# Decoder layer on one core: the last two steps of the feed-forward network interleaved by token tile, with the last layer norm and the store done tile by tile

## What is computed

```python
x = _layernorm(x + attention(x, Wq, bq, Wk, bk, Wv, bv, Wo, bo))      # 16 heads, rope, causal
x = _layernorm(x + cross(x, ctx, Wq, bq, Wk, bk))                     # softmax(q k^T) over the context, applied to x
gate = einsum('bsd,hd->bsh', x, w_gate)                               # d = 512, h = 2048
up = einsum('bsd,hd->bsh', x, w_up)
gated = silu(gate) * up
x = _layernorm(x + einsum('bsh,dh->bsd', gated, w_down))
```

## Time and profile before

| What | Value |
|---|---|
| Median of 3 runs | 1050.85 us (1048.11, 1050.85, 1050.95) |
| The profiled execution's own time | 1048.29 us |
| Its span | 1046.5 us |
| TensorE busy in the span | 94% |
| Mean granted TensorE clock | 0.978 of full speed |
| VectorE, ScalarE, GpSimd busy | 60%, 47%, 34% |

### The profile page before, as it was taken

How to read it: one execution, slowest core, us unless ns; L and a number is a source line. 1 busy time by engine, 2 the same in 40 slices (tenths; PEclk the granted TensorE clock), 3 DMA queues, 4 the chain that set the end, 5 groups by cost and what they waited for, 6 DMA issues and landing times.

```text
span 1046.5 us, 15709 instructions
## 1 busy us (share of the span) xinstructions
PE 981.5 (94%) x5416; PEld 794.5 (76%) x5416; DVE 630.3 (60%) x1344; ACT 493.5 (47%) x1075; POOL 352.3 (34%) x353
## 2 busy tenths in 40 slices
PE   7688999999999868899999999999999999999995
PEld 5556777777777656688888788888788888788884
DVE  5577788878778766545544475544565444653343
ACT  5476767777767654344432334432334432333330
POOL 2566646655756521213111132012132112131112
PEclk9899999999999979899999999999999999999998
DMA  6966676855868730262222143222252221242301
GB/s 219 255 152 168 171 183 158 229 142 145 242 158 191 186 120 1 91 230 91 73 79 91 61 175 148 91 73 80 78 207 98 91 91 61 91 171 92 111 9 41
DMA packets 44862, 134.53 MB, mean 129 GB/s; under 512 B 5232, under 2 KB 5360, under 8 KB 41968
## 3 DMA queue, kind: packets, MB, share of 16 engines
q1 hardware_dynamic: 44784, 133.52, 42.1%
HBM read 104.14 MB, written 25.17 MB: 124 GB/s over the span
## 4 chain that ended last, share of the span: by engine, by line
PE 79%; ACT 6%; DVE 5%; issue 5%; POOL 2%; DMA 2%; SPq 1%; POOLq 0%; DVEq 0%; ACTq 0%
PE pu L523 17%; PE pg L523 17%; PE pd L523 16%; PE pj L478 11%; PE pj L523 5%; PE pv L514 4%; PE ps L489 3%; PE pa L502 2%; ACT prob L678 2%; PE pb L502 2%; DVE prob L874 2%; PE pj L529 1%; ACT pT L685 1%; PE pj L476 1%; DMA ks<-qk_scratch 1%
## 5 line engine op out<-in xcount | busy, mean ns | idle before, releaser
L1191 POOL TENSOR_TENSOR g_lo<-gated,g_hi 128x512 fp32r<-128x512 f32 x64 | 82.5, 1289 | 439.8 <-ACT g_hi L769 439.8
L678 ACT ACTIVATE prob<-prob,nmax 128x512 f32<-128x512 f32 (+3 forms) x256 | 143.7, 562 | 114.4 <-DVE nmax L874 114.2
L874 DVE CUSTOM_DVE_ANT_0 prob<-ps,mask 128x512 f32<-128x512 f32 (+3 forms) x256 | 122.8, 484 | 79.8 <-PE ps L489 76.0
L980 DVE TENSOR_TENSOR dn_lo<-f_raw,dn_hi 128x512 fp32r<-128x512 f32 x64 | 51.2, 801 | 121.2 <-ACT dn_hi L753 121.2
L489 PE MATMUL ps<-ks,qs 128*128 128x256 f32 (+2 forms) x256 | 107.0, 420 | 13.5 <-DMA ks<-qk_scratch 8.0
L1001 DVE SCALAR_TENSOR_TENSOR half<-th,pg 128x512 f32<-128x512 f32 x64 | 43.9, 687 | 104.4 <-ACT th L760 104.4
L523 PE MATMUL pd<-dn_hi,g_hi 128*128 128x512 f32 x256 | 101.2, 395 | 0.2 <-POOL g_lo L1191 0.2
L760 ACT ACTIVATE th<-pg 128x512 f32<-128x512 f32 x64 | 38.3, 598 | 131.6 <-PE pg L523 131.6
L523 PE MATMUL pd<-dn_lo,g_hi 128*128 128x512 f32 x256 | 99.8, 390 | 0.0
L523 PE MATMUL pd<-dn_hi,g_lo 128*128 128x512 f32 x256 | 99.6, 389 | 0.0
L769 ACT CAST g_hi<-gated 128x512 fp32r<-128x512 f32 x64 | 39.7, 620 | 120.4 <-DVE gated L1008 120.4
(11 more groups left out here) (162 smaller groups left out, 2226.4 us busy)
## 6 DMA issues: line engine op xcount, KB each, us to landing
f_raw<-in_w_ffn SPq DMA_DIRECT2D x64, 768.0 KB, 4.3
qs<-qk_scratch SPq DMA_DIRECT2D x64, 256.0 KB, 4.8
ks<-qk_scratch SPq DMA_DIRECT2D x64, 256.0 KB, 7.8
qk_scratch<-qk_hi SPq DMA_DIRECT2D x32, 256.0 KB, 2.0
qk_scratch<-raw SPq DMA_DIRECT2D x32, 256.0 KB, 2.1
res<-in_x SPq DMA_DIRECT2D x4, 1024.0 KB, 4.9
x_scratch<-res SPq DMA_DIRECT2D x4, 1024.0 KB, 5.8
x<-x_scratch SPq DMA_DIRECT2D x4, 1024.0 KB, 4.8
```

The costliest lines, as they stand in the source:

```text
L678: act.activation(prob[:, t % PROBS, 0:w], prob[:, t % PROBS, 0:w], ACT.Exp, bias=nmax[:, n % 2, i:i + 1], scale=-1.0, accum_out=rsum[:, n ...
L874: dve.tensor_tensor_reduce(prob[:, t % PROBS, 0:w], ps[:, t % 2, 0:w], mask[:, S - w:S], -D ** -0.5, 3e38, ALU.add, ALU.min, accum_out=nma ...
L980: dve.tensor_tensor(dn_lo[:, i % 2, :], f_raw[i % NR][:, 2 * KT * P:], dn_hi[:, i % 2, :].bitcast(F32), ALU.subtract).then_inc(dnlo_done, 1)
L1191: pool.tensor_tensor(g_lo[:, i % 2, :], gated[:], g_hi[:, i % 2, :].bitcast(F32), ALU.subtract).then_inc(glo_done, 1)
```

## The change

Four edits, all at the end of the fourth sequence.

1. PE's order. The loop of steps ends at i = 61. Then `hidden` of steps 62 and 63 run one behind the other, then `down(61)`, and then the down products of steps 62 and 63 in turn, token tile by token tile: 3 matmuls of step 62 and 3 of step 63 finish a tile and raise `tile_full`.
2. Banks and buffers. The gate and up products of step 63 go to the two banks of `pj`, which nothing uses any more at that time, and not to `pg` and `pu`. The halves of the gated activation and of the down weights of step 63 have buffers of their own, `last_hi` and `last_lo`. `gu_half(63)` moves from the midst of step 62 to the end of step 61, on ACT and DVE.
3. Layer norm. The sum and the moments of a tile wait for that tile's `tile_full` and not for the whole `d_full`. POOL makes -mean*rstd (`nmr2`) for tiles 0 to 2 by one more instruction each, and ACT normalizes these three tiles; DVE normalizes only tile 3.
4. Store. SP issues one store of 256 KB for each tile in place of one of 1 MB.

```diff
+    last_hi, last_lo, nmr2 = sb("last_hi", [P, 2, S], F32R), sb("last_lo", [P, 2, S], F32R), sb("nmr2", [P, ST])
...
+    def gate_bank(i):
+        return pj[:, 0, :] if i == STEPS - 1 else pg[:]
+    def up_bank(i):
+        return pj[:, 1, :] if i == STEPS - 1 else pu[:]
+    def gated_halves(i):
+        return (last_hi[:, 0, :], last_lo[:, 0, :]) if i == STEPS - 1 else (g_hi[:, i % 2, :], g_lo[:, i % 2, :])
+    def down_halves(i):
+        return (last_hi[:, 1, :], last_lo[:, 1, :]) if i == STEPS - 1 else (dn_hi[:, i % 2, :], dn_lo[:, i % 2, :])
...
@@ SP @@
-            sp.wait_ge(ln_done[1], ST * (b + 1))
-            sp.dma_start(out[b * P:(b + 1) * P, :], fin[:]).then_inc(out_done, 16)
-        sp.wait_ge(out_done, 16 * B)
+            if not last:
+                sp.wait_ge(ln_done[1], ST * (b + 1))
+                sp.dma_start(out[b * P:(b + 1) * P, :], fin[:]).then_inc(out_done, 16)
+        for s in range(ST):
+            if s < ST - 1:
+                sp.wait_ge(tile_done, s + 1)
+            else:
+                sp.wait_ge(ln_done[1], ST * (B - 1) + 1)
+            sp.dma_start(out[(B - 1) * P:B * P, s * E:(s + 1) * E], fin[:, s, :]).then_inc(out_done, 16)
+        sp.wait_ge(out_done, 16 * (B - 1 + ST))
...
@@ PE @@
+        def last_down(i, s):
+            if s == 0:
+                pe.wait_ge(dnlo_done, i + 1)
+                pe.wait_ge(glo_done, i + 1)
+            cols = slice(s * P, (s + 1) * P)
+            return three(pd[:, s, :], 1, lambda k: [g[:, cols] for g in gated_halves(i)],
+                         lambda k: down_halves(i), False, i == STEPS - 1)
-        for i in range(1, STEPS):
+        for i in range(1, STEPS - 2):
             hidden(i, 0)
             hidden(i, 1)
...
             down(i - 1)
-        down(STEPS - 1)
+        for i in (STEPS - 2, STEPS - 1):
+            hidden(i, 0)
+            hidden(i, 1)
+        down(STEPS - 3)
+        for s in range(ST):
+            last_down(STEPS - 2, s)
+            last_down(STEPS - 1, s).then_inc(tile_full, 1)
...
@@ ACT, step (DVE's the same) @@
-            if i < STEPS - 1:
+            if i < STEPS - 2:
                 gu_half(i + 1)
...
             if i < STEPS - 1:
                 dn_half(i + 1)
+            if i == STEPS - 3:
+                gu_half(i + 2)
...
@@ ACT, behind the last step @@
+        for s in range(ST - 1):
+            act.wait_ge(nmr2_done, s + 1)
+            act.activation(fin[:, s, :], fin[:, s, :], ACT.Identity, bias=nmr2[:, s:s + 1],
+                           scale=rstd2[1][:, s, :]).then_inc(tile_done, 1)
...
@@ DVE @@
         def finished(b, s):
             if s == 0:
                 dve.wait_ge(fin_in, 16 * (b + 1))
+            if b == B - 1:
+                dve.wait_ge(tile_full, s + 1)
+            elif s == 0:
                 dve.wait_ge(d_full, HT * (b + 1))
...
-        for s in range(ST):
-            normalized(B - 1, 1, fin, s)
+        normalized(B - 1, 1, fin, ST - 1)
...
@@ POOL @@
             root(B - 1, 1, s)
+            if s < ST - 1:
+                pool.wait_ge(rstd2_done[1], ST * (B - 1) + s + 1)
+                pool.tensor_scalar(nmr2[:, s:s + 1], mv2[1][:, s, 0:1], rstd2[1][:, s, :], -1.0, ALU.mult, ALU.mult).then_inc(nmr2_done, 1)
```

More of the change, by code:

```diff
@@ L588, in hidden @@
                     pe.wait_ge(max_done, SCORES)
-                else:
+                elif i < STEPS - 1:
                     pe.wait_ge(gate_read, i)
-            elif i:
+            elif 0 < i < STEPS - 1:
                 pe.wait_ge(gated_done, i)
-            three((pg, pu)[u][:], KT, lambda k: (gu_hi[:, i % 2, u, k, :], gu_lo[:, i % 2, u, k, :]),
+            three((gate_bank, up_bank)[u](i), KT, lambda k: (gu_hi[:, i % 2, u, k, :], gu_lo[:, i % 2, u, k, :]),
                   lambda k: (x2T_hi[:, k, :], x2T_lo[:, k, :])).then_inc((g_full, u_full)[u], 1)
@@ L750, in dn_half @@
                 act.wait_ge(av_done, GROUPS)
-            if i >= 2:
+            if 2 <= i < STEPS - 1:
                 act.wait_ge(d_full, i - 1)
-            act.copy(dn_hi[:, i % 2, :], f_raw[i % NR][:, 2 * KT * P:]).then_inc(dnhi_done, 1)
+            act.copy(down_halves(i)[0], f_raw[i % NR][:, 2 * KT * P:]).then_inc(dnhi_done, 1)
         def step(i):
@@ L759, in step @@
                 act.wait_ge(gate_read, i)
-            act.activation(th[:], pg[:], ACT.Tanh, scale=0.5).then_inc(th_done, 1)
-            if i < STEPS - 1:
+            act.activation(th[:], gate_bank(i), ACT.Tanh, scale=0.5).then_inc(th_done, 1)
+            if i < STEPS - 2:
                 gu_half(i + 1)
@@ L766, in step @@
             act.wait_ge(gated_done, i + 1)
-            if i >= 2:
+            if 2 <= i < STEPS - 1:
                 act.wait_ge(d_full, i - 1)
-            act.copy(g_hi[:, i % 2, :], gated[:]).then_inc(ghi_done, 1)
+            act.copy(gated_halves(i)[0], gated[:]).then_inc(ghi_done, 1)
             if b < B - 1:
@@ L977, in dn_half @@
             dve.wait_ge(dnhi_done, i + 1)
-            if i >= 2:
+            if 2 <= i < STEPS - 1:
                 dve.wait_ge(d_full, i - 1)
-            dve.tensor_tensor(dn_lo[:, i % 2, :], f_raw[i % NR][:, 2 * KT * P:], dn_hi[:, i % 2, :].bitcast(F32),
+            hi, lo = down_halves(i)
+            dve.tensor_tensor(lo, f_raw[i % NR][:, 2 * KT * P:], hi.bitcast(F32),
                               ALU.subtract).then_inc(dnlo_done, 1)
@@ L1000, in step @@
                 dve.wait_ge(gated_done, i)
-            dve.scalar_tensor_tensor(half[:], th[:], 1.0, pg[:], ALU.add, ALU.mult).then_inc(gate_read, 1)
-            if i < STEPS - 1:
+            dve.scalar_tensor_tensor(half[:], th[:], 1.0, gate_bank(i), ALU.add, ALU.mult).then_inc(gate_read, 1)
+            if i < STEPS - 2:
                 gu_half(i + 1)
@@ L1007, in step @@
                 dve.wait_ge(glo_done, i)
-            dve.scalar_tensor_tensor(gated[:], half[:], 0.5, pu[:], ALU.mult, ALU.mult).then_inc(gated_done, 1)
+            dve.scalar_tensor_tensor(gated[:], half[:], 0.5, up_bank(i), ALU.mult, ALU.mult).then_inc(gated_done, 1)
             steps = BESIDE.get(j, []) if b < B - 1 else []
@@ L1188, in step @@
             pool.wait_ge(ghi_done, i + 1)
-            if i >= 2:
+            if 2 <= i < STEPS - 1:
                 pool.wait_ge(d_full, i - 1)
-            pool.tensor_tensor(g_lo[:, i % 2, :], gated[:], g_hi[:, i % 2, :].bitcast(F32), ALU.subtract).then_inc(glo_done, 1)
+            hi, lo = gated_halves(i)
+            pool.tensor_tensor(lo, gated[:], hi.bitcast(F32), ALU.subtract).then_inc(glo_done, 1)
             if b < B - 1:
```

3 lines of the change are left out of this document (2 added, 1 removed).

## The result

The change ran at a median of 1043.65 us (4 runs, 1041.40 to 1044.61) against 1050.46 us for the kernel before (4 runs). The ratio is 0.993, with a 95% interval of 0.9907 to 0.9953: faster, by 0.7%. The forecast was 1044.0. In a later comparison, eleven runs of before against five of the change (a sixth, disturbed, took 5522 us and is left out), the ratio was 0.992 (0.9904 to 0.9935).

What follows compares the result with a forecast made beforehand. TensorE was taken as busy 94% near full clock, so only the end behind the last shared work counted. Terms 4.53 + 0 + 0.43 + 1.8 = 6.8 us, from median 1050.85 to 1044.0 us; range 1040.9 to 1046.4.

Steps and rivals of the forecast that it cites:

- two levels 2.7 us apart: Runs of before: three and the profiled one fall in two pairs; the change not showing because of this or a small gain, 8%.
- other stages that move: Sign of being wrong: stages moved which the change gives no reason for.
- Term 1: First tile whole: DVE's first sum starts at 1029.53 and not at 1034.06, 4.53 us earlier, if nothing waits.
- The slack of 0.36 us: Step 63's `gated`, `g_hi`, `g_lo` chain is ready 0.36 us before PE's fourth end matmul; beyond that, each us late costs one.
- The place of `gu_half(63)`: Step 63's weight halves, made behind `dn_hi(62)`, are done at 1017.45; PE wants them at 1019.75, slack 2.3 us.
- Term 2: DVE's four sums and moments still need 6.21 us, slower than PE's tiles: no gain, no loss.
- The met waits: DVE's four new waits are met when it comes to them; cost between 0 and 0.3 us in all, taken as 0.
- Term 3: Last tile's norm: from `veps` start to norm end 1.44 us, not 1.87; gain 0.43 us, 0 if POOL stays slow.
- the change without term 3: Gain 6.4 us if the last norm brings nothing; part of a rival (term 3 or 4 nothing, or late handover), chance 12%.
- Term 4: Last store of 256 KB lands after 2.1 us, where 1 MB took 3.9: gain 1.8 us, bounds 0 and 1.9.
- The rival that the stores queue up: Four stores of 2.1 us each go strictly one after another: gain 4.5 us, median 1046.3, chance 8%.
- The rival of the falling clock: Dense end of 84 matmuls granted 1.2 GHz, not 2.4: result 12.2 us slower, 1063.0, chance 2%.

Runs made afterwards that it cites:

- The run step by step: The change, but TensorE runs the last two down products one behind the other, not in turn: tail 27.58 us, 1.97 later than the change.
- norms on VectorE: The change, but VectorE normalizes all four tiles and SP stores each as it is ready: tail 26.74 us, median 1045.86 us, ratio 0.9959.
- The single edit undone: The change, but with one store of 1 MB at its end in place of four: tail 27.32 us, 1.71 later; median 1046.16 us, ratio 0.9966.
- a burst: The change, but all four 256 KB stores are issued one behind the other when tile 3 is ready: tail 27.82 us, 2.2 later than the change.
- the run with the old buffers: The change, but step 63's halves use the old pairs of buffers and wait until down(61) has read them: tail 31.92 us, one run 1050.21 us.
- the change again: The change itself once more, against before on the same chip, in more rounds: tail 25.59 us, median 1041.67 against 1050.42 us, ratio 0.992.

## Why the prediction was right

**What bounds.** Right in its cut: nothing ahead of step 62 was touched, and all of the gain lies in the tail. Wrong in how it read the runs: it saw two levels 2.7 us apart in four runs. The 25 runs of before that stood beside the first experiments lie everywhere between 1048.0 and 1052.6 us. The profiled execution of before was at the low end of that, and carrying the gain over to the median was still the right step.

How close the median came is in part luck. The tail shrank by 6.58 us and the median by 6.81, with an interval of 4.9 to 9.8 us by the ratio; in the later comparison the medians were 8.75 us apart. The forecast of a span near 1039.7 us missed in the first profile (1042.4) and held in the second (1039.6). In the first the head was 2.5 us longer than before's, and the prediction had named other stages that move as a sign of being wrong; the second shows that the head scatters by that much without a change of code. What bears the forecast out is the tail and its terms.

**Term 1**, 4.53 us forecast: the first sum moved from 19.75 to 15.23 us behind the start of step 62, 4.52. The run step by step parts it: 2.0 for taking steps 62 and 63 in turn, and 2.5 for the signal at each tile and the closed gap. No run parts the 2.5; by the rows of before, 9 matmuls are 2.04 of it and the gap and restart 0.45. The slack of 0.36 us was measured at 0.36. The place of `gu_half(63)` cost nothing: `gu_lo` ended at 1019.83, and PE wanted it 24 matmuls behind 1016.79, at 1022.2. Of the two sorts of room that step 63 got, the banks did nothing, and everything hung on the buffers: without them term 1 turns into a wait of 4.2 us and a slower clock. The prediction called both free and did not say that only one was needed.

**Term 2**, 0 forecast: from 1032.02 to the end of the last moments at 1038.23 are 6.21 us, as before. The met waits cost nothing that can be seen; DVE, not PE, sets the pace of the tiles.

**Term 3**, 0.43 forecast: from the start of `veps` to the end of the norm 1.44 us, as forecast, with 0.21 and 0.56 for the pair. That the slow pair goes with DVE's normalizations is shown by the runs that keep them (0.41 and 0.79 in both). The Trainium skill's rule of the shared ports ("SBUF — State Buffer", "SBUF: two separate sides") would do this, and the traces here agree; that it is the ports was not separated from another cause.

The number was right, but the slow pair is only part of the reason. The prediction read DVE as waiting for POOL's last `rstd`. The timeline of before up to 1041.65 us shows DVE at work on the three norms ahead of that one:

```profile
1040.17 1.43 DVE L965 TENSOR_SCALAR fin<-fin,mv,rstd 128x512 f32<-128x512 f32 x3
```

They end at 1041.60, and the fourth starts at 1041.67. The first three start 0.43 and 0.46 us apart, so with a fast pair the fourth could have started at about 1041.52. That makes an estimated gain of 0.15 us and not 0.43: two things of nearly the same length ended together, and the change takes both away. No run has ACT's norms with a slow pair, so how much the norms taken off DVE would bring by themselves is not shown.

What the term missed is the second effect of the sharing: it spaces the stores, worth another 0.7 us, which the prediction had counted under term 4 by taking them to be 1 to 1.5 us apart. So the change without term 3 was priced at a gain of 6.4 us, and norms on VectorE measures 32.19 - 26.74 = 5.45.

**Term 4**, 1.8 forecast: from the end of the norm to the end of the span 2.66 us, and 4.28 before: 1.62. The single edit undone gives 1.7. The landing is 2.2 us and not 2.1. The rival that the stores queue up had its price from strict order, and it does not hold: from the first issue of a burst to the end of the span are 4.8 us. The rule of the Trainium skill ("DMA: Bandwidth & Descriptors", "Bandwidth") to batch to 1 MiB holds for the burst, by 0.5 us, and misleads where three quarters of the store can go early. The prediction's 2.6 us for a quarter came from a fit that the same page of the Trainium skill ("Anatomy of one DMA") gives for DMAs that GpSimd issues; these stores are issued by SP, and the trace has 2.2.

**Sum**: 6.8 forecast, 6.58 measured in the tail. The rival of the falling clock did not happen in the change. It did happen in the run with the old buffers, and there it followed a wait, not the dense stretch that the rival had feared.

## What to carry over

The end of a kernel has no later work to hide in, so it pays to finish outputs one by one: let the last two accumulation steps run output tile by output tile, signal each tile, and let the next engines and the store follow. Reordering that brings two producers together needs buffers of its own for the second, and here the wait that they avoid also costs the clock. Split a store only if its first parts can leave while there is other work; issued together, the parts are worse than the whole. Who does the work ahead of the stores matters for them too: 0.8 of the 1.7 us that the split brings here hang on ACT's norms, which set the stores 0.9 to 1.5 us apart.

## What the hardware showed that I had not expected

**The head's spread arises in two stretches, the first of them by the clock.** Two executions of the same kernel, the change and the change again, have heads 2.8 us apart (1016.79 and 1014.01). Set side by side row by row on ACT and DVE, they are within 0.02 us of each other from 60 to 88 us. From 95 to 365 us the second is 1.6 us ahead, from 434 us on 3.0, and at the start of the tail 2.8. For instance the first tanh behind 460 us in the change, and the same one in the change again:

```profile
460.80 0.60 ACT L800 ACTIVATE th<-pg 128x512 f32<-128x512 f32 x1 [2.09 <-PE pg L548]
...
457.76 0.60 ACT L800 ACTIVATE th<-pg 128x512 f32<-128x512 f32 x1 [2.10 <-PE pg L548]
```

The two places (columns as above), the change:

```profile
85.00:90.00 5.00, 4.41 (x16) 3.23 (x15) 2.34 (x9) 4.32 (x12) 2.87 (x3) 0.50 0.65 213
90.00:95.00 5.00, 5.00 (x68) 3.40 (x66) 2.34 (x6) 0.81 (x2) 1.53 (x2) 0.82 1.06 228
350.00:450.00 100.00, 79.52 (x514) 61.99 (x513) 64.61 (x166) 47.15 (x118) 29.04 (x41) 0.88 0.32 100
```

The change again:

```profile
85.00:90.00 5.00, 4.43 (x24) 3.04 (x22) 2.96 (x12) 4.38 (x13) 2.87 (x3) 0.69 0.66 205
90.00:95.00 5.00, 5.00 (x74) 3.93 (x74) 2.31 (x7) 2.30 (x8) 1.72 (x2) 1.00 1.08 236
350.00:450.00 100.00, 80.51 (x518) 63.15 (x518) 64.97 (x164) 47.12 (x118) 28.62 (x43) 0.88 0.30 96
```

In the five us before 85 PE was busy for only 2.80 us in the first execution and for 2.98 in the second, and in both the granted clock fell (0.65 and 0.62 over those five). In the first it stayed at the lower level, 1.2 GHz, through all of 85 to 90 us (0.50) and into the next five (0.82), with PE busy 4.41 and 5.00 us of them; in the second it was back at 2.4 GHz by 90 (0.69, then 1.00). Two times five us at 0.19 and 0.18 less are an estimated 1.85 us of PE at full clock, where 1.6 are seen, so here the clock is enough. The other 1.4 us arise between 365 and 434 us, where the clock goes up and down in both and its mean is the same, 0.88; how they come about is not shown.

**Two subtractions side by side.** In the change DVE's split of step 63's down weights lies beside POOL's `g_lo` of step 62, both with two SBUF inputs. DVE's, which started second, took 1.36 us:

```profile
1023.85 1.30 POOL L1243 TENSOR_TENSOR g_lo<-gated,g_hi 128x512 fp32r<-128x512 f32 x1 [6.87 <-ACT g_hi L809]
...
1024.33 1.36 DVE L1030 TENSOR_TENSOR last_lo<-f_raw,last_hi 128x512 fp32r<-128x512 f32 x1 [1.21 <-ACT last_hi L793]
```

It cost nothing here, since DVE's next instruction waited for the tanh anyway. It is not new either. In the kernel before, DVE's split of the down weights ran 64 times. With nothing on POOL beside it, it took 0.69 us (49 times); when POOL began something while it ran, 0.67 to 0.69 (4 times); when a subtraction of POOL's was running already, 0.83 to 2.24 (11 times), each time ending 0.55 us behind POOL's. One of the longest, in the timeline of before:

```profile
471.63 2.40 POOL L1162 TENSOR_TENSOR c_lo<-c_raw,c_hi 128x1024 fp32r<-128x1024 f32 x1
...
472.34 2.24 DVE L980 TENSOR_TENSOR dn_lo<-f_raw,dn_hi 128x512 fp32r<-128x512 f32 x1 [2.69 <-ACT dn_hi L753]
```

The one that starts second pays: here it is DVE, and in term 3, where DVE's norm had started first, it was POOL, by 0.2 us an instruction.
